# Keeping the residual in the output tensor and adding the down projection to it by accumulating transfers

## The reference, cut to what matters

```
x = x + xattn(layernorm(x), ctx, ctx, Wq, Wo)            # x is [4, 2048, 512] fp32; the result is called x1
xq = fake_quant(layernorm(x1), clip_x)                   # int8 levels, one scale for the whole tensor
h = fake_quant(silu(xq @ gate.T) * (xq @ up.T), clip_down)   # [.., 1408]; one scale for the whole tensor
out = x1 + h @ down.T
```

## Time and profile before

| | |
|---|---|
| median of the 3 runs | 1118.85 us |
| the profiled execution, its own time | 1118.99 us |
| its span, first to last instruction | 1117.2 us |
| mean granted TensorE clock | 0.998 |
| PE busy | 1095.0 us, 98% of the span |
| DVE, ACT, POOL busy | 798.1, 622.6, 385.4 us |
| memory read, written | 137.15 MB, 72.51 MB |

### The profile page before, as it was taken

One profiled execution on the slowest core, in us unless ns is written; L12 is line 12 of the kernel. 1 busy time (PEld: TensorE's weight loads), 2 busy tenths in 40 slices (PEclk: granted clock), 3 DMA queues, 4 the chain that ended last, 5 costly groups with the idle time before them and its releaser, 6 DMA issues. The chain is left out here.

```text
span 1117.2 us, 17314 instructions
## 1 busy us (share of the span) xinstructions
PE 1095.0 (98%) x6203; PEld 616.9 (55%) x6203; DVE 798.1 (71%) x1411; ACT 622.6 (56%) x765; POOL 385.4 (34%) x317
## 2 busy tenths in 40 slices
PE   8899999999999999999999899999999999999988
PEld 6656666666666666666665544444444444444433
DVE  6867777777767676766555667777787877686667
ACT  4376655565555555555445266565657564865350
POOL 6565444464444544444321000000000000375655
PEclk9999999999999999999999999999999999999999
DMA  7334766676555555543137356766666502999995
GB/s 270 116 100 132 197 177 162 176 194 179 161 146 173 158 161 148 172 143 92 61 103 237 128 191 215 248 229 237 240 230 246 179 20 94 366 411 428 426 419 217
DMA packets 122613, 223.00 MB, mean 200 GB/s; under 512 B 59168, under 2 KB 68000, under 8 KB 110624
## 3 DMA queue, kind: packets, MB, share of 16 engines
q1 hardware_dynamic: 122528, 221.89, 59.6%
HBM read 137.15 MB, written 72.51 MB: 188 GB/s over the span
## 5 line engine op out<-in xcount | busy, mean ns | idle before, releaser
L799 PE MATMUL a_Q<-a_xT,wq 128*128 128x512 f32 x768 | 193.1, 400 | 2.6 <-DVE a_q L641 2.6
L444 POOL TENSOR_TENSOR a_aT<-a_att,a_aT 128x512 fp32r<-128x512 f32 x64 | 82.7, 1292 | 299.5 <-ACT a_aT L517 299.5
L952 ACT ACTIVATE e_sg<-e_G,x_gus 128x512 f32<-128x512 f32 x176 | 119.0, 685 | 114.7 <-PE e_G L1045 114.7
L1008 DVE SCALAR_TENSOR_TENSOR h<-e_U,x_gus,e_sg 128x512 f32<-128x512 f32 x176 | 131.9, 749 | 70.2 <-PE e_U L1049 44.2
L1049 PE MATMUL e_U<-e_cT,gu 128*128 128x512 bf16 x704 | 180.7, 379 | 0.0
L1045 PE MATMUL e_G<-e_cT,gu 128*128 128x512 bf16 x704 | 180.7, 379 | 0.0
L1155 POOL TENSOR_TENSOR x<-x,c_y 128x512 f32<-128x512 f32 x32 | 51.7, 1646 | 365.5 <-DVE c_y L1184 355.1
L761 PE MATMUL a_O<-a_wo,a_aT 128*128 128x512 f32 x720 | 175.4, 392 | 0.0
L799 PEld LDWEIGHTS a_Q<-a_xT,wq 128*128 128x128 f32 x768 | 139.3, 188 | 54.4 <-issue 27.3
L1228 PE MATMUL c_Y<-dn,gu 128*128 128x512 bf16 x660 | 143.8, 379 | 5.2 <-DVE gu L1177 5.2
L761 PEld LDWEIGHTS a_O<-a_wo,a_aT 128*128 128x128 f32 x720 | 132.2, 188 | 28.1 <-issue 2.9
(11 more groups left out here) (142 smaller groups left out, 1347.5 us busy)
## 6 DMA issues: line engine op xcount, KB each, us to landing
x<-x_d SPq DMA_DIRECT2D x24, 1024.0 KB, 6.3
h_d<-h SPq DMA_DIRECT2D x24, 1024.0 KB, 4.1
h<-h_d SPq DMA_DIRECT2D x11, 1536.0 KB, 17.3
a_xr<-in_x SPq DMA_DIRECT2D x64, 256.0 KB, 3.4
a_xt<-in_xT SPq DMA_DIRECT2D x64, 256.0 KB, 4.0
x_d<-a_xr SPq DMA_DIRECT2D x64, 256.0 KB, 2.6
a_xs<-in_x SPq DMA_DIRECT2D x60, 256.0 KB, 3.7
h<-h_d SPq DMA_DIRECT2D x11, 1280.0 KB, 19.9
```

The lines of the kernel that those rows point to most:

```text
L444: nc.gpsimd.tensor_tensor(aT[:, n.par, 1, n.g], att[:], aT[:, n.par, 0, n.g].bitcast(F32), ALU.subtract).then_inc(aT_l, 1)
L799: mm = nc.tensor.matmul(Q[:], wq[:, wp, j, P * n.g:P * (n.g + 1)], xT[:, n.par, xp, j], start=(ins == 0), stop=(ins == 3 * KT - 1))
L952: nc.scalar.activation(sg[:, s], G[:, t % GU], ACT.Silu, scale=gus[:, t:t + 1]).then_inc(silued, 1)
L1008: nc.vector.scalar_tensor_tensor(out=h[:, place(u, p), t], in0=U[:, t % GU], scalar=gus[:, IT + t:IT + t + 1], in1=sg[:, s], op0=ALU.mult, ...
```

## The change

The internal tensor `x1_d` goes. The name now stands for the output tensor itself, seen in the same shape: x1 is written there by `attend` and read from there by `expand`. In `contract` nothing loads the residual any more. DVE scales a tile of `c_Y` straight into the ring, and GpSimd's queue, instead of adding, issues one transfer per block that adds the ring's block to the output in memory (`accum_op`), and four smaller ones for the last block. The buffer `c_y`, the semaphores `added`, `last_added` and `x1_in` of this stage, the two loads at the end of `expand`, and DVE's additions for the last block go too. DVE's new wait is for the transfer of block k-4, before it writes to that place of the ring.

```diff
--- before.py
+++ after.py
@@ -100,7 +100,6 @@
 
 def xattn_ffn(nc, x, xT_all, ctxT, WqT, WoT, clip_x, clip_down, w_gate, w_up, w_down, ident, headmask, negsel, out):
     dram = lambda n, s, dt: nc.dram_tensor(n, s, dt, kind="Internal").ap()
-    x1_d = dram("x1_d", [BLOCKS, P, TT, D], F32)
     h_d = dram("h_d", [BLOCKS, P, IT * TOK], F32)
     gu_d = dram("gu_d", [2 * IT, P, D], BF16)
     dn_d = dram("dn_d", [KT, P, INNER], BF16)
@@ -108,7 +107,7 @@
     rs_d = dram("rs_d", [BLOCKS, TT, P], F32)
     x_t = x.rearrange("b (n p t) d -> (b n) t p d", t=TT, p=P)
     x_k = xT_all.rearrange("(k p) (b t) -> b k p t", p=P, t=TOK)
-    out_t = out.rearrange("b (n p t) d -> (b n) p t d", t=TT, p=P)
+    x1_d = out.rearrange("b (n p t) d -> (b n) p t d", t=TT, p=P)
 
     with ExitStack() as top:
         keep = lambda n, s, dt=F32: top.enter_context(nc.sbuf_tensor(n, s, dt))
@@ -150,7 +149,7 @@
             hmax = keep2("hmax", [P, IT])
             h = keep2("h", [P, 1 + BLOCKS - HELD_FROM, IT, TOK])
             expand(nc, x1_d, h_d, gu, c8, sg, x1, h, hmax, mom, sig, wscale, id32, id16, x1_out, x1_in, gu_in)
-            contract(nc, h_d, x1_d, out_t, gu, dn, h, x1, hmax, sig, dscale, id32, dn_in, ds_in)
+            contract(nc, h_d, x1_d, gu, dn, h, x1, hmax, sig, dscale, id32, dn_in, ds_in)
 
 
 class Item:
@@ -916,11 +915,6 @@
                 run(sp, blk)
 
                 for p in range(2):
-                    sp.wait_ge(coded, (BLOCKS - 1 + p) * TT)
-                    sp.dma_start(x1[:, p], x1_d[ORDER[p]]).then_inc(x1_in[p], 16)
-                for p in range(2):
-                    sp.wait_ge(x1_in[p], 16 * (BLOCKS // 2 + 1))
-                for p in range(2):
                     sp.wait_ge(h_out[p], 16 * len(CHUNKS) * HELD_FROM // 2)
 
             @block.scalar
@@ -1072,7 +1066,7 @@
                 warm(WARM_END)
 
 
-def contract(nc, h_d, x1_d, out_t, gu, dn, h, x1, hmax, sig, dscale, id32, dn_in, ds_in):
+def contract(nc, h_d, x1_d, gu, dn, h, x1, hmax, sig, dscale, id32, dn_in, ds_in):
 
     with ExitStack() as st:
         sb = lambda n, s, dt=F32: st.enter_context(nc.sbuf_tensor(n, s, dt))
@@ -1084,15 +1078,12 @@
         c8 = sb("c_c8", [P, 2, IT, TOK], I8)
         cb = gu[:].rearrange("p t k n -> p (t k n)").rearrange("p (b t n) -> p b t n", b=2, t=IT)
         z = sb("c_z", [P, 2, TT, D])
-        y = sb("c_y", [P, 2, D])
         Y = ps("c_Y", [P, 2 * TT, D])
         s_tmax, s_gmax, s_hinv, s_own = (sem("h_" + n) for n in ("tmax", "gmax", "hinv", "own"))
         h_in = [[sem(f"c_h_in{n}{b}") for b in range(NH)] for n in range(2)]
-        x1_in = [sem(f"c_x1_in{r}") for r in range(4)]
         y_out = [sem(f"c_y_out{r}") for r in range(4)]
         last_out = sem("c_last_out")
-        coded, cast, downed, scaled, added, last_added = (sem("c_" + n) for n in (
-            "coded", "cast", "downed", "scaled", "added", "last_added"))
+        coded, cast, downed, scaled = (sem("c_" + n) for n in ("coded", "cast", "downed", "scaled"))
         CH = ((0, 6), (6, IT))
         FIRST_CH = ((0, 1), (1, 2), (2, 4), (4, 6), (6, 8), (8, IT))
         LAST = BLOCKS - 1
@@ -1113,46 +1104,24 @@
 
             @block.sync
             def _(sp):
-                def load_x1(k):
-                    sp.dma_start(ring(k), x1_d[ORDER[k]]).then_inc(x1_in[k % 4], 16)
-
-                load_x1(2)
-                load_x1(3)
-                for k in range(BLOCKS + 1):
-                    if k < BLOCKS - NH:
-
-                        for n, (a, e) in enumerate(CH):
-                            sp.wait_ge(coded, upto(k, e))
-                            sp.dma_start(h[:, BUFFER[k], a:e].rearrange("p t n -> p (t n)"),
-                                         h_d[ORDER[k + NH], :, TOK * a:TOK * e]).then_inc(h_in[n][k % NH], 16)
-                    if k >= 2:
-                        sp.wait_ge(added, (k - 1) * TT)
-                        sp.dma_start(out_t[ORDER[k - 2]], ring(k - 2)).then_inc(y_out[(k - 2) % 4], 16)
-                    if 3 <= k < LAST:
-
-                        sp.wait_ge(y_out[(k - 3) % 4], 16 * ((k - 3) // 4 + 1))
-                        load_x1(k + 1)
-
-                for t in range(TT):
-                    sp.wait_ge(last_added, t + 1)
-                    sp.dma_start(out_t[ORDER[LAST], :, t], ring(LAST)[:, t]).then_inc(last_out, 16)
+                for k in range(BLOCKS - NH):
+
+                    for n, (a, e) in enumerate(CH):
+                        sp.wait_ge(coded, upto(k, e))
+                        sp.dma_start(h[:, BUFFER[k], a:e].rearrange("p t n -> p (t n)"),
+                                     h_d[ORDER[k + NH], :, TOK * a:TOK * e]).then_inc(h_in[n][k % NH], 16)
                 for r in range(4):
                     sp.wait_ge(y_out[r], 16 * len(range(r, LAST, 4)))
                 sp.wait_ge(last_out, 16 * TT)
 
-            def residual_in(eng, k):
-
-                if k >= 2:
-                    eng.wait_ge(x1_in[k % 4], 16 * (k // 4 + (k % 4 >= 2)))
-
             @block.gpsimd
             def _(pool):
                 for k in range(LAST):
-                    residual_in(pool, k)
-                    for t in range(TT):
-                        i = k * TT + t
-                        pool.wait_ge(scaled, i + 1)
-                        nc.gpsimd.tensor_tensor(ring(k)[:, t], ring(k)[:, t], y[:, i % 2], ALU.add).then_inc(added, 1)
+                    pool.wait_ge(scaled, (k + 1) * TT)
+                    nc.gpsimd.dma_start(x1_d[ORDER[k]], ring(k), accum_op=ALU.add).then_inc(y_out[k % 4], 16)
+                for t in range(TT):
+                    pool.wait_ge(scaled, LAST * TT + t + 1)
+                    nc.gpsimd.dma_start(x1_d[ORDER[LAST], :, t], ring(LAST)[:, t], accum_op=ALU.add).then_inc(last_out, 16)
 
             @block.scalar
             def _(act):
@@ -1179,15 +1148,10 @@
                 def scale(k):
                     for t in range(TT):
                         i = k * TT + t
-                        after(dve, added, min(i - 1, LAST * TT), 1 << 30)
+                        if t == 0 and k >= 4:
+                            dve.wait_ge(y_out[k % 4], 16 * (k // 4))
                         dve.wait_ge(downed, i + 1)
-                        nc.vector.tensor_tensor(y[:, i % 2], Y[:, TT * (k % 2) + t], dns[:], ALU.mult).then_inc(scaled, 1)
-                        if k == LAST:
-                            dve.wait_ge(scaled, i + 1)
-                            if t == 0:
-                                residual_in(dve, k)
-                            nc.vector.tensor_tensor(ring(k)[:, t], ring(k)[:, t], y[:, i % 2], ALU.add).then_inc(last_added, 1)
-                            dve.wait_ge(last_added, t + 1)
+                        nc.vector.tensor_tensor(ring(k)[:, t], Y[:, TT * (k % 2) + t], dns[:], ALU.mult).then_inc(scaled, 1)
 
                 own.step(nc.vector.tensor_reduce(tmax[:], hmax[:], AX.X, ALU.max))
                 nc.vector.memset(gmax[:], 0.0).then_inc(s_tmax, 1)
```

## The result

The changed kernel takes 1122.35 us (median of 7 runs, 1121.28 to 1123.04) where the kernel before takes 1118.26 us (median of 7 runs; the 3 of the table of before are among them). The ratio is 1.0035, with a 95% interval of 1.0024 to 1.0047: slower by about 4 us. The profiled execution took 1121.79 us; its span is 1119.9 us, before it was 1117.2. Its mean granted TensorE clock is 0.998, as before; in the six other executions it is 0.995 to 0.997, so in them the clock was low in some stretch that no trace shows.

The account below looks back on a forecast made before the run. The prediction took full DMA engines, with TensorE close behind, to bound the last stage. From a span of 1117.2, -6.0 + 5.2 + 2.8 gave 1119.2, and 1.8 around it 1121.0 us; the range ran from 1113.5 to 1146.

Parts of the forecast that it names:

- likeliest case: The case with an addition priced at 4.92 us and served ahead of h: 1118 to 1123 us, chance 0.33.
- same: Band of 1116.6 to 1121.1 us that a measurement cannot tell from no change; chance 0.23.
- What bounds the kernel: Last stage: a block needs 11.7 us of full DMA engines, TensorE 9.50; the change removes a dependency, no byte of reads.
- The first part: Residual loads, GpSimd's additions and the wait on them go; TensorE's six gaps from 1060 us close: -6.0 us.
- The second part: Price of an accumulating transfer of 1024 KB: 4.92 us of the engines, as load plus store; bounds 2.46 and 7.4.
- The third part: Additions in their own queue are served ahead of h; last h lands at 1099.9, TensorE ends at 1112.2: +5.2 us.
- The fourth part: After TensorE's end, scaling, issue and the last accumulating transfer take 7.0 us instead of 4.2: +2.8, bounds -0.4 and +4.6.
- no backlog stands at the end: The engines' total work finishes at 1109.7 us, so no transfers are left piled up at the end.
- The fifth part: x1's earlier stores and loads moving to the output tensor, and two loads ending the second stage: counted at nothing.
- Half shares: Rival: h keeps half of the engines, lands at 1093, TensorE ends at 1107.0; 1115.8 us, chance 0.15.
- A cheap addition: Rival: an addition costs near 2.46 us, a block 9.2 us of transfers, h is early; 1113.8 us, chance 0.15.
- A dear one: Rival: an addition costs over 5.1 us and transfers alone set the end; 1132 us at price 6, chance 0.37.

Follow-up runs that it names:

- Run 10: The kernel before, with seven tiles of `c_y` instead of two, residual loads, additions and stores as they were: 1112.68 us, ratio 0.9953.
- run 4: The changed kernel, but GpSimd issues block k's addition only when h load k+3 (or the last) has landed: 1119.07 us, ratio 1.0014.
- run 1: The changed kernel with GpSimd's transfers storing the scaled tile over x1 without adding, the sum left out: 1112.85 us, ratio 0.9952.
- run 3: The changed kernel without the 22 reloads of h, so 11 blocks use the wrong h: 1114.6 us in one execution.
- run 5: The changed kernel with blocks 0 and 1 as before (residual loaded early, added on GpSimd, stored from SP's queue): 1117.18 us, ratio 0.9991.
- run 6: The changed kernel with block 14 scaled on DVE between the two casts of block 15, not behind both: 1121.54 us, ratio 1.0027.
- run 7: The changed kernel with only block 15 as before (residual loaded behind the last h, added on DVE, stored from SP's queue): 1119.5 us, ratio 1.0014.
- run 2: The kernel before with x1 kept in the output tensor (`x1_d = out_t`) and nothing else changed: 1118.34 us, ratio 1.000.

## Why the prediction was right, and where it was not

The forecast was 1121.0 us, with 1118 to 1123 for its likeliest case; 1122.35 came. The time lies outside the band that the prediction called "same" (to 1121.1), on the slower side, to which it gave 0.52. The distance was undersized: +2.0 over the profiled execution before, against +2.8 between the two profiled executions and +4.1 between the medians.

**What bounds the kernel** held. The DMA engines stay full, at a share of 1.02, and the change removed a dependency and none of the engines' work. Run 10 shows the first half by itself: with the same transfers and no dependency the 6.0 us are gone (5.3 by the ratio).

**The first part** (-6.0 for the old gaps) came exactly: no gap before 1078 us, and casts of 1.75 and 1.5 us as taken.

**The second part**, the price, was taken as 4.92 us between 2.46 and 7.4 and measured as 4.95 back to back (run 4) and 5.0 in the mix. It is the price of two copies, a load and a store: run 1 takes the adding and its second read out, and 9.3 us go. The Trainium skill's ratio of 1.93, measured there on a collective's adding step (Collectives: The Full Stack, section "The bandwidth ceiling: the fold count and why AG ≠ RS ≠ AR"), agrees nearly; the measurement of 2.0 decides, and lies on the side of the load and store that the rows had shown.

**The third part** (+5.2 for late h) was measured as +5.7. The last piece of h was predicted for 1099.9 and released ScalarE at 1099.06, in a stage that began 1.3 us earlier. From the first addition on h got 60.5 us of work in 130, 46.5% of the engines; what the additions had, 69.6 us, is 14 of them at 4.95, the number forecast. The sum asked only that the additions get their whole demand, 52%, and they did. Its words "served ahead" are not borne out: beside h an addition took 13.6 and 14.1 us to land, and with the engines to itself 8.4 (run 3), so h had its turns in between. By what rule the two queues take turns cannot be told. Runs 4 and 5 confirm the mechanism from both sides, by sequence and by amount. The detail was off: ScalarE waits for h in twelve conversions from 1017 us on, not in the last two or three blocks. Its lead and DVE's hid these waits until 1078.

**The fourth part** failed in size: the end was taken as +2.8 and came as +4.2 (8.4 us after TensorE's end, not 7.0). Two errors are in it, and they partly cancel, which is luck. The terms were too large: in run 6, without the backlog, the last addition takes 4.7 us from the start of its issue to the end of the span, not 1.6 + 4.6, and the whole end 5.7. And 2.7 us of backlog were left out. The step that was wrong is "no backlog stands at the end". The engines' total was right, but the sum assumed that block 14's addition starts 2.4 us after its matmuls. It starts 7.4 us after them, because on DVE block 14's scaling stands behind a cast that waits for the last h. So the engines idle from 1102 to 1106 and then have 10 us of additions to do. Run 6 undoes that (5.7 us), run 7 takes block 15's additions out of the end (4.1), and run 3, with no h at all, has 6.7. The sign "the last accumulating transfer 4 to 5 us from issue to landing" failed with it: a median of 8.2.

**The fifth part** was right for the place of x1 (run 2), and wrong for the two loads at the end of the second stage. They cost nothing where they stood, as it said; what it left out is that their 2 x 2.46 us come back inside the full stage as the second reads of two additions. The third part's sum contains them, but the sentence that put them at nothing hides the cheapest repair (run 5).

**The rivals.** Half shares, with h at 1093, did not come. A cheap addition would have given 1113.8 by my reckoning; run 1 shows that case at 1112.85. A dear one decides from 5.1 us; at 4.95 the kernel stands just below the point. Of 4.1 us of loss, the end's 4.2 and the new gaps' 5.7 stand against the 6.0 of the old gaps.

## What to carry to other kernels

Adding in memory by a transfer removes a wait, a buffer and an engine's work, but its engines' time is that of the load and the store together (4.95 us against 2 x 2.46 for 1024 KB): where DMA is full, as here, it buys nothing but the dependency, and it pushes the read to the latest moment, out of any idle stretch in which it could have been prefetched. Ask first whether the wait it removes is one of order; here seven buffers instead of two took the same 6 us at no cost (0.9953). In this kernel accumulating transfers did not pay for the blocks whose residual can be loaded while the engines are idle, nor at the very end: keeping the first two and the last block out of them turned a loss of 4 us into a gain of 3.6.

## What the runs showed of the hardware

- The profile's bytes count an accumulating transfer once. What it costs besides shows only in the busy share: 311 GB/s at a share of 1.02, where copies gave 426 at 1.01; alone and back to back 212 GB/s at 1.03.
- GpSimd's issue of a transfer is held up by a cast on DVE. Alone, an accumulating one takes 0.86 us (a plain one 0.54, run 1). Beside a cast it ends just after the cast (1.49 us, accumulating or plain). On DVE and GpSimd of the changed kernel:

```profile
982.86 3.19 DVE L1146 CAST gu<-c_c 128x3072 bf16<-128x3072 int8 x2
```

```profile
983.24 1.49 POOL L1121 DMA_DIRECT2D out<-c_z  x1 [8.01 <-DVE c_z L1154]
```

The first of the two casts, 1.75 us long, ends at 984.61 and the issue at 984.73. In the one case where the issue began 0.1 us later after the cast's start, at 1030.82 for a cast from 1030.34, it took 1.41 us and ended at 1032.23, again 0.14 us after the cast. The casts do not become longer by it: 1.75 and 1.5 us on average, where the additions on GpSimd had stretched them to 2.14 and 2.48. The Trainium skill (SBUF — State Buffer, section "Who interferes with whom") says that DVE and GpSimd share a pair of SBUF ports, that a cast can be run in a mode that takes this pair, that whoever issues first then holds it for its whole instruction, and that GpSimd lacks it meanwhile for generating the descriptors of its transfers. For the issues these rows agree; which mode the casts ran in they do not say. In mid-stage this held nobody up: DVE never waited for the ring in this trace.
- After an idle stretch of TensorE the granted clock sometimes fell to its lower level. After 3.32 us (run 6) and 3.25 us (run 7) it was 0.56 and 0.55, and the next 38 matmuls took 10.06 and 11.13 us instead of 8.38; after 2.31 us (run 4), behind 84 us without a gap, it was 0.50 for 3.4 us and cost 1.6 us. After 2.54 us in the changed kernel, where 6 matmuls and 0.57 us of idle time stood just before, and after gaps of 1.84 us and less elsewhere, it stayed at 1.00. So the length of the gap alone does not decide, and what does these traces do not show. A repair can lose part of its gain that way, as in runs 4, 6 and 7.
